# Causal attention in a two-layer model: zeros written into the probabilities in place of masks added to the scores

## The reference

```python
q = _heads(x @ Wq + bq); k = _heads(x @ Wk + bk); v = _heads(x @ Wv + bv)   # 16 heads of 16
att = jnp.einsum('bhqd,bhkd->bhqk', q, k) * scale
causal = jnp.tril(jnp.ones((T, T), bool))
att = jnp.where(causal[None, None], att, -jnp.inf)
y = jnp.einsum('bhqk,bhkd->bhqd', jax.nn.softmax(att, axis=-1), v)
```

## Time and profile before

| | us |
|---|---|
| median of three runs | 1774.21 (1771.69 to 1776.6) |
| profiled execution | 1775.95 |
| its span, first to last instruction | 1774.2 |
| mean granted clock of TensorE, share of full speed | 0.916 |

### The profile page before, as it was taken

How to read it: one execution, slowest core, us unless ns; L and a number is a source line. 1 busy time by engine, 2 the same in 40 slices (tenths; PEclk the granted TensorE clock), 3 DMA queues, 4 the chain that set the end, 5 groups by cost and what they waited for, 6 DMA issues and landing times.

```text
span 1774.2 us, 31229 instructions
## 1 busy us (share of the span) xinstructions
PE 1550.6 (87%) x11094; PEld 664.0 (37%) x11094; DVE 1325.8 (75%) x2583; ACT 1133.0 (64%) x2178; POOL 464.8 (26%) x677
## 2 busy tenths in 40 slices
PE   3998889988998989988998989998988997888677
PEld 1344335423442334323542335323543442232226
DVE  5787766788678777887687866878578687788287
ACT  1374576566756686666665775667655854866497
POOL 3211413330323122421333122421342222310130
PEclk8788979998999989998998989989998898899898
DMA  6322201212121212121121212121121011011313
GB/s 184 94 83 91 87 19 44 70 45 66 35 76 46 63 43 64 52 76 42 38 77 35 61 43 64 52 75 49 58 64 37 27 55 40 25 56 42 143 60 120
DMA packets 115018, 110.99 MB, mean 63 GB/s; under 512 B 21552, under 2 KB 108720, under 8 KB 114864
## 3 DMA queue, kind: packets, MB, share of 16 engines
q1 hardware_dynamic: 114864, 108.99, 20.6%
HBM read 69.35 MB, written 38.80 MB: 61 GB/s over the span
## 4 chain that ended last, share of the span: by engine, by line
PE 55%; DVE 19%; ACT 13%; issue 5%; POOL 3%; DMA 2%; SPq 2%; ACTq 0%; POOLq 0%; DVEq 0%
PE acc L1633 14%; PE st L1619 10%; DVE nmax L1372 9%; PE misc L1563 8%; PE misc L1535 6%; PE misc L1589 5%; ACT probs L1053 5%; PE misc L1660 3%; PE misc L1575 3%; ACT tail_h L1123 2%; DMA stack<-nrow 2%; PE misc L1600 2%; PE misc L1687 2%; ACT tail_h L1108 1%; DVE hid L1321 1%
## 5 line engine op out<-in xcount | busy, mean ns | idle before, releaser
L1372 DVE TENSOR_REDUCE nmax<-misc 128x1 f32<-128x512 f32 (+3 forms) x1408 | 856.4, 658 | 250.1 <-PE misc L1600 127.3
L1053 ACT ACTIVATE probs<-st 128x512 f32<-128x512 f32 (+3 forms) x1536 | 742.6, 548 | 316.6 <-PE st L1619 213.6
L1619 PE MATMUL st<-stack 50*128 50x512 f16 (+3 forms) x1536 | 458.0, 377 | 68.5 <-ACT probs L1053 54.6
L1589 PE MATMUL misc<-stack 48*128 48x512 f16 (+3 forms) x1536 | 483.2, 377 | 38.6 <-DVE nmax L1372 30.8
L1619 PEld LDWEIGHTS st<-stack 50*128 50x128 f16 x1536 | 110.9, 95 | 460.2 <-ACT probs L1053 263.2
L1633 PE MATMUL acc<-probs,v_x 128*32 128x512 f32 x1152 | 178.5, 696 | 0.0
L1589 PEld LDWEIGHTS misc<-stack 48*128 48x128 f16 x1536 | 125.8, 95 | 110.9 <-DVE nmax L1372 82.2
L1039 ACT ACTIVATE qk<-misc,b 128x512 f32<-128x512 f32 x96 | 65.9, 687 | 149.8 <-PE misc L1563 149.6
L932 POOL TENSOR_TENSOR parts<-qk,zero 128x512 f16<-128x512 f32 x78 | 81.1, 1040 | 297.6 <-ACT qk L1039 297.5
L1633 PE MATMUL acc<-probs,v_s 128*32 128x512 f32 (+3 forms) x1152 | 117.7, 482 | 0.1
L1633 PE MATMUL acc<-probs,v_f 128*32 128x512 f32 x768 | 111.3, 654 | 0.0
(11 more groups left out here) (282 smaller groups left out, 2090.9 us busy)
## 6 DMA issues: line engine op xcount, KB each, us to landing
parts_xk<-parts SPq DMA_DIRECT2D x36, 128.0 KB
parts_xq<-parts SPq DMA_DIRECT2D x36, 128.0 KB
stack<-parts_xq SPq DMA_DIRECT2D x72, 64.0 KB, 2.1
stack<-parts_xk SPq DMA_DIRECT2D x72, 64.0 KB, 2.1
xn_A<-in_x_dram SPq DMA_DIRECT2D x8, 512.0 KB, 4.3
hid<-in_L_ffn_w_dram SPq DMA_DIRECT2D x4, 1024.0 KB, 5.4
parts_sk<-parts SPq DMA_DIRECT2D x32, 128.0 KB
parts_sq<-parts SPq DMA_DIRECT2D x32, 128.0 KB
```

The source lines that it names most:

```text
L1053: act.activation(probs[:, j % P_SLOTS, c, T - w:], st_bank(n, 4 * j + c)[:, 0:w], ACT.Exp, scale=scale_of[s.unit[1]]).then_inc(exp_done, 1)
L1372: dve.tensor_reduce(nmax[:, ring, first:first + NT * (len(cs) - 1) + 1:NT], src, AX.X, ALU.max, negate=True).then_inc(misc_free[slot], 1)
L1589: last = pe.matmul(o, stack[rows, r, 0, c // 2, P * i:P * i + P], stack[rows, r, 1, c // 2, 0:w], start=True, stop=not causal)
L1619: last = pe.matmul(o[:, 0:w], stack[rows, r, 1, c // 2, P * j:P * j + P], stack[rows, r, 0, c // 2, T - w:T], start=True, stop=not causal)
```

## The change

The scores of causal units get no mask any more: `scores` on PE is one matmul in place of three. The exponential is taken of everything, future keys of the diagonal block included. A new step `mask` stands after the scores of each key tile of a causal unit, ahead of the values of the tile before. In it Pool waits for the four exponentials of the tile and writes zeros into the part above the diagonal, with one `affine_select` in place over 128 keys x 4 heads x 128 queries of float32. The values of a causal unit wait for this step (`probs_masked`) where they waited for the exponentials. The maxima keep their masks. The two mask constants of the scores and what made them are gone. The output is meant to be the same.

```diff
             if last_run and u[1] == "s":
@@ -145,6 +145,8 @@
                 out.append(("scores", u, j, d))
                 out += maxima[HU * j + d]
             last_run = c + RUN == HU
+            if last_run and u[1] == "s":
+                out.append(("mask", u, j))
             if last_run and j:
                 out.append(("values", u, j - 1))
             if last_run and j == 0 and prev:
@@ -440,8 +442,7 @@
...
-        mask_st, mask_mx, identb_x, mask_st_x, mask_mx_x = \
-            (lb(n, [P, P], BF16) for n in ("mask_st", "mask_mx", "identb_x", "mask_st_x", "mask_mx_x"))
+        mask_mx, identb_x, mask_mx_x = (lb(n, [P, P], BF16) for n in ("mask_mx", "identb_x", "mask_mx_x"))
...
@@ -846,35 +848,29 @@
...
-            for n, t_ in enumerate((ident, identb, identh, mask_st, mask_mx, identb_x, mask_st_x, mask_mx_x)):
+            for n, t_ in enumerate((ident, identb, identh, mask_mx, identb_x, mask_mx_x)):
-            keep(mask_st, 1, 0, consts_made)
-            keep(mask_st_x, 1, -HALF, zeroed)
-            pool.memset(mask_st_x[HALF:, :], 0.0).then_inc(zeroed, 1)
-            keep(mask_st_x, 1, HALF, consts_made)
...
@@ -944,6 +940,14 @@
                 pool.wait_ge(negmax_split, done.at(2))
                 pool.tensor_tensor(part[1], most, part[0], ALU.subtract).then_inc(negmax_split, 1)
 
+            def mask(s):
+
+                j, g = s.args[0], s.unit[2]
+                pool.wait_ge(exp_done, s.n.times(16, 4 * j + 4 + ST_BANKS).at())
+                own = probs[:, j % P_SLOTS, :, P * j:P * j + P]
+                pool.affine_select(out=own, in_=own, compare_op=ALU.is_ge, fill=0.0, base=0,
+                                   pattern=[[0, HU], [1, P]], channel_multiplier=-1).then_inc(probs_masked, 1)
+
             def y_T(s):
                 if s.args[0] == "A":
                     wait_misc_read(pool, s, 0, ("heads_out", (s.key[1], "s", NU - 1)))
@@ -1609,17 +1613,14 @@
 
             def scores(s):
                 (j, c), n, r = s.args, s.n, s.n.slot(STACKS)
-                causal = s.unit[1] == "s"
-                w = T - P * j if causal else T
+                w = T - P * j if s.unit[1] == "s" else T
                 if (j, c) == (0, 0):
                     pe.wait_ge(negmax_landed[n.slot(2)], n.round(2).times(32, 64).at())
                 o = st_bank(n, 4 * j + c)
                 pe.wait_ge(exp_done, n.times(16, 4 * j + c + 1).at())
                 rows = rows_of(c, AUG)
                 last = pe.matmul(o[:, 0:w], stack[rows, r, 1, c // 2, P * j:P * j + P], stack[rows, r, 0, c // 2, T - w:T],
-                                 start=True, stop=not causal)
-                if causal:
-                    last = masked(o[:, 0:P], c, (mask_st, mask_st_x), (slice(0, HALF), slice(0, P)))
+                                 start=True, stop=True)
                 last.then_inc(st_full, 1)
 
             def values(s):
@@ -1628,7 +1629,10 @@
                 if j == 0:
                     pe.wait_ge(v_done[p], s.b.times(2, 2).at())
                     pe.wait_ge(heads_full, n.at(1))
-                pe.wait_ge(exp_done, n.times(16, 4 * j + 4 + ST_BANKS).at())
+                if p == "s":
+                    pe.wait_ge(probs_masked, s.b.times(NU * NT, NT * g + j + 1).at())
+                else:
+                    pe.wait_ge(exp_done, n.times(16, 4 * j + 4 + ST_BANKS).at())
                 for c in range(HU):
                     last = pe.matmul(acc[32 * c:32 * c + 32, T - w:T], v_of(s, p)[:, j, HU * g + c, :],
                                      probs[:, j % P_SLOTS, c, T - w:T], start=j == 0, stop=j == NT - 1)
```

More of the change, by code:

```diff
@@ L517, in two_layers_kernel @@
         NFIRST = 6
-        NMADE = 17
+        NMADE = 15
         consts_in, consts_made = sem("consts_in"), sem("consts_made")
@@ L526, in two_layers_kernel @@
         st_full, exp_done = sem("st_full"), sem("exp_done")
+        probs_masked = sem("probs_masked")
         values_done = sem("values_done")
@@ L854, in _ @@
                                    pattern=[[-1, P]], channel_multiplier=1).then_inc(ident_made, 1)
-            pool.wait_ge(zeroed, 8)
+            pool.wait_ge(zeroed, 6)
             def keep(t_, sign, base, made):
@@ L860, in keep @@
                                    pattern=[[sign, P]], channel_multiplier=-sign).then_inc(made, 1)
-            keep(mask_st, 1, 0, consts_made)
             keep(mask_mx, -1, 0, consts_made)
             for n, base in enumerate((HALF, -HALF)):
-                pool.wait_ge(zeroed, 8 + n)
+                pool.wait_ge(zeroed, 6 + n)
                 pool.affine_select(out=identb_x[:, :], in_=identb_x[:, :], compare_op=ALU.not_equal, fill=1.0, base=base,
                                    pattern=[[-1, P]], channel_multiplier=1).then_inc(*((zeroed, 1) if n == 0 else (consts_made, 1)))
-            keep(mask_st_x, 1, -HALF, zeroed)
-            pool.wait_ge(zeroed, 10)
-            pool.memset(mask_st_x[HALF:, :], 0.0).then_inc(zeroed, 1)
-            pool.wait_ge(zeroed, 11)
-            keep(mask_st_x, 1, HALF, consts_made)
             keep(mask_mx_x, -1, -HALF, zeroed)
-            pool.wait_ge(zeroed, 12)
+            pool.wait_ge(zeroed, 8)
             pool.memset(mask_mx_x[0:HALF, :], 0.0).then_inc(zeroed, 1)
-            pool.wait_ge(zeroed, 13)
+            pool.wait_ge(zeroed, 9)
             keep(mask_mx_x, -1, HALF, consts_made)
@@ L965, in down_q @@
                 pool.tensor_tensor(hq[:, t % 2, :], hid[:, t, :], magic[:, :].to_broadcast([P, F]), ALU.subtract).then_inc(hq_full, 1)
-            walk(pool, dict(consts_rest=consts_rest, stats=stats_, norm=norm, mid_bias=mid_bias, project=project, negmax=negmax,
+            walk(pool, dict(consts_rest=consts_rest, stats=stats_, norm=norm, mid_bias=mid_bias, project=project, negmax=negmax, mask=mask,
                             y_T=y_T, hid_scale=hid_scale, down_q=down_q))
```

## The result

The changed kernel takes a median of **1781.91 us** over six runs. Five of them lie between 1778.27 and 1787.07, with a median of 1781.54; the sixth took 1960.75 at a mean granted clock of 0.697 and is left out of the ratio. Six runs of the kernel before beside it took 1772.95 (1768.03 to 1776.6). The ratio is 1.0054, 95% interval 1.0029 to 1.0079: **slower by half a per cent, where the forecast was 0.4% faster**. The profiled execution took 1781.45 us with a span of 1779.6.

The account below looks back on a forecast made before the run. PE was fullest (87% busy, 55% of the chain), with different limits per causal unit. Gain 15.2 less loss 8.5 is 6.7 us: 1775.95 to 1769.2 profiled, median 1767.5; forecast 1762 to 1772, whole range 1752 to 1784.

Parts of the forecast that it names:

- The gain, 15.2 us: Mask matmuls leaving PE in causal units: their chain share, 7.1 us in batches 1 to 5, 8.1 in 0, 6, 7.
- The selection, 0.65 us: Each of 128 selections on Pool takes 0.65 us, interpolated between two profile rows; bounds 0.29 and 1.17.
- The late selection of s1: Tile 1 behind the next batch's statistics: values 0.98 us late, cost 0, as PE idles for the maxima's transfer anyway.
- The late selections of s2: Tile 1 behind a split, 0.87 us late, costs 0.2; tile 3 late too, an estimated 0.5.
- The late selection of s3: Tile 2 behind a split: values 1.56 us late, costing 0.6 a batch.
- DVE has a backlog ...; I let it hide 1.0: In s3, DVE's queued maxima were taken to hide 1.0 of the 1.56 us late start.
- The whole loss, 8.5 us: Late selections: 1.3 us a batch, 6.5 for batches 1 to 5, plus 1.0 each for batches 0 and 7.
- rival B: Selections queued behind splits in s2 and s3 count in full: 10 us slower, 1784; chance 0.17.
- somewhat under half of the forecast: Part of the forecast's 0.45 chance counted, with D (nothing moves) and half of C, into 0.30 for no change.
- The net, -6.7 us: Whole kernel: gain 15.2 less loss 8.5, giving a median of 1767.5 us.
- Rival C: More PE idling ahead of s2 lowers TensorE's clock in four more batches: 9.3 us, net 2.6 slower, 1777; chance 0.11.
- The units x and f as they were: Expected sign in the profile after: units x and f, outside the causal ones, unchanged.

Follow-up runs that it names:

- experiment 1: Kernel before with the score masks removed and no selection on Pool, so future keys are not zeroed: 1764.22 us, ratio 0.9947.
- the row first: In s1 of batches 1 to 5 SP issues the transfer of s2's row of maxima between queries and keys; on the kernel before alone, 1766.35 us.
- experiment 7: Kernel before, masks kept, with SP sending s2's row of maxima earlier in s1 of batches 1 to 5: 1766.35 us, ratio 0.998.
- experiment 10: Kernel before without score masks or selections, and SP sending s2's row of maxima earlier in s1: 1748.54 us, ratio 0.9879.
- experiment 13: Changed kernel with Pool's selection of tile 1 in s1 ahead of the next batch's statistics, batches 1 to 5: 1783.98 us, ratio 1.0077.
- experiment 12: Changed kernel, batches 1 to 5: s3's tile 2 selection before the split, s1's tile 1 before the statistics, s2's row of maxima sent earlier: 1760.96 us.
- experiment 3: Changed kernel with Pool's selection of tile 2 in s3 ahead of the split, batches 1 to 5: 1771.59 us, ratio 0.9984.
- experiment 2: Kernel before with its masks kept and the selections and the values' wait for Pool added: 1786.48 us, ratio 1.0078.
- experiment 4: Changed kernel with PE's masks kept and no selection in 24 of 128 key tiles, where Pool was late: 1770.76 us, ratio 0.9995.

## Why the prediction was wrong, point by point

**The gain, 15.2 us: right.** 15.2 at equal clock (experiment 1), 15.9 with the row first. s0 gave 1.02 us against 0.95 in four of the five middle batches (in batch 1 the clock fell, see above), s1 nothing that shows, or 0.2 with the row first (11.76 and 11.58), and s3 0.33 (12.34 and 12.01) against 0.07. That the sum agrees to a tenth is in part luck: in batch 7, where experiments 7 and 10 have all four causal units at the full clock, they differ by 1.33 us (56.26 and 54.93) where 2.8 were counted. Still, reading the chain unit by unit came out near 15 where the busy time was 186 us.

**The selection, 0.65 us: right,** 639 ns. Of the bounds (0.29 and 1.17) neither was near. Between 128 elements (292 ns) and 512 (637 ns, the median) the runs show (637 - 292) / 384 = 0.90 ns for each. By the GPSIMD Engine Reference of the Trainium skill (7, Performance pitfalls for Q7 kernels) an element would take 1.7 or 0.86 ns, as estimates from its two figures and its 1.2 GHz; the trace is near the faster one, beside a fixed part of some 0.18 us.

**The late selection of s1, nothing: right** (experiment 13), and for the reason given. The falls that go with it (12 of 35 batches) were not in the prediction; in the profiles of the changed kernel they are 1 of 10.

**The late selections of s2, 0.7 us a batch: nearly right.** PE waits 0.75 us at tile 1 and 0.35 at tile 3. The first is covered, as foretold (0.2): with the row first s2 is 14.10 us with it and 13.96 without (experiments 12 and 10, means of five). The second falls into s3, which is 12.43 us with it and 12.01 without (experiments 3 and 1), 0.4 where 0.5 was estimated.

**The late selection of s3, 0.6 us: too low.** The wait was foretold (1.52 against 1.56), its cost was not: without a fall the pair of s3 and f0 takes 29.31 us with it and 28.45 without (experiment 3), 0.86 more. The step "DVE has a backlog ...; I let it hide 1.0" hid too much, since 0.66 is hidden. In the stalled stretch the chain passes from PE's scores to ACT's exponentials, and ACT idles 2.43 us, DVE 0.76. Over five batches that term is 4.3, not 3.0.

**The whole loss, 8.5 us: right in sum,** 7.9 at equal clock (experiment 2): the terms are each within 1.3 us. In batch 7 s3 is 1.25 us longer than without selections (15.69 against 14.44), in batch 0 the causal units are the same with and without; 1.0 each was assumed.

**The range.** The measured time lies near the 1784 of rival B, but not by its mechanism: B priced the late selections at 25 us, and they cost 7.9. Of the chances, "somewhat under half of the forecast" does not give the 0.30 for no change: 0.12 and half of 0.11 leave 0.125, which is 28% of 0.45.

**The net, -6.7 us: at equal clock -5.0. The step that failed is the sum itself:** "Gain 15.2 - 8.5 = 6.7 us" is carried from the old time to the new one as if the clock stayed as it was. It has no term for **the granted clock**, which is 0.9055 in the mean of 17 runs against 0.9207. At 10.1 us for 0.01 that is 15 us, as much as the gain, and -5.0 + 15.4 is the 10 us measured. Rival C was this mechanism, but it stood in one place only (ahead of s2), was priced at 9.3 us, and had a chance of 0.11. The runs show four places:
- Ahead of s2, where PE waits for SP (experiments 1 and 4). In the changed kernel this adds nothing: the late selection of s1 takes up part of that pause, and only batch 4 has a long s2, 15.21 us, as batch 5 had before.
- Behind the stall in s3, where the falls strike f0 (ten of twenty pairs with the stall, five of ten in the changed kernel). "The units x and f as they were" was therefore wrong.
- In s0 of batch 1. It takes 23.5 us at a clock of 0.85 in ten of the twelve profiles without score masks in it, 20.3 at 1.00 in the two others (experiments 4 and 10), and 21.2 at 1.00 in the three with masks.
- In s1, behind the late selection (12 of 35 batches).

The page of the Trainium skill which bears on it, TensorE: Matmul & The Clock Gate (HAM oscillation — how this bites in real kernels), describes waits for transfers between stretches of matmuls that lower the clock for the stretch behind them. The trace agrees where a fall came (ahead of s2 in experiment 1), and shows falls behind waits for Pool as well; but half of the stalls in s3 have none behind them.

**Not settled.** Which pause lowers the clock: the same 1.52 us in s3 did in batch 3 and not in batch 4, 1.5 us ahead of s2 did in experiment 1 and not in 13 (batch 3 of both), and the 2.2 us in s0 of batch 1 did in ten profiles and not in five. And the two parts do not add up in the clock: the removal alone and the addition alone lower it by 0.006 each, both together by 0.015. That PE is less full *and* stalled more would fit, but it is not shown: no experiment separates the two.

**The profile that was read.** The profiled execution of the kernel before had a clock of 0.916, on the low side of its runs (mean 0.9207), which fits its 1775.95 us, 1.7 above the median. The prediction took that offset off again, and it plays no part in the miss.

## What to carry to other kernels

Take work from the fullest engine only together with what it waits for next: here the removal alone paid 9.5 us, and 17.8 once a transfer was issued 2 us earlier. A step that is put into an in-order queue must be placed against each neighbour: five selections of 128 stood behind a split and made the difference between slower and level, while moving the others ahead put off stores and cost 11 us. And compare kernels by time and mean granted clock together; a difference of 0.015 in the clock went with 15 us, as much as all the masks that were removed.

## What the runs showed of the hardware

The clock of TensorE is not a constant offset: in 106 runs of one kernel it ranged from 0.912 to 0.932, and 0.01 went with 10 us, 0.6% of the time.

Of the 128 selections one meets a DVE instruction with two SBUF inputs. It is not slowed; DVE is. Timeline of the changed kernel:

```profile
1460.94 0.64 POOL L948 TENSOR_SCALAR_AFFINE_SELECT probs<-probs 128x512 f32<-128x512 f32 x1 [3.76 <-ACT probs L1057]
1460.95 1.16 DVE L1217 TENSOR_TENSOR parts<-qk,parts 128x512 f16<-128x512 f32 x1
```

Pool began 0.01 us earlier and took its usual time, DVE's subtraction took 1.16 us where it takes 0.69. The prediction put that price on Pool. The SBUF page of the Trainium skill (Who interferes with whom) has the two exclude each other; in these rows, and in the earlier trace rows, where DVE was first, the one that started first kept its time. It is one case each way. The one selection that took more than 647 ns, 793 in batch 0, also began while DVE was at work, 0.91 us into a one-input instruction over 2,048 elements that kept its usual 1.21 us.
